# Five engine orders instead of one: a per-engine order table, and waits moved to the first instruction that needs them

## The chip, the cores and the metric

One core of one Trainium2 chip. It has a matrix engine (TensorE, "PE", its weight loads "PEld"), a vector engine (VectorE, "DVE"), a scalar engine (ScalarE, "ACT"), a general engine (GpSimd, "POOL") and a queue engine (SyncE, "SP") that here only issues DMAs. The engines run side by side, each through its own fixed list of instructions, and meet only at semaphores. The metric is the device time of one execution in microseconds, median of several runs.

## The reference

The input x is 4 items of 256 tokens by 256 channels; each item has a context `ctx_1024` (256 x 128) and a side input. Four layers of gated cross attention and gated feed-forward follow. What each stage of the kernel computes for one item b:

```
s0     x += tanh(g0) * mamba(ctx, gate = layernorm(x))      # conv, softplus step, 16 states of a linear
                                                           # recurrence over 256 tokens, 256 channels
h1,r1  h = layernorm(x); route to 2 of 8 experts (softmax, top 2)
s1     x += tanh * (8 experts of width 176 weighted by the routing, and a shared one of 352), SwiGLU
s2     x += tanh * two smooth-quantised (int8-like) matmuls against the side input and the context
s3     x += tanh * ternary-weight SwiGLU, width 1024
s4,sa  x += tanh * attention, 16 heads of 128, keys and queries rms-normed, 256 context tokens
s5     x += tanh * ternary-weight SwiGLU with activations quantised to 8 bits and a norm between
s6     x += tanh * attention whose queries and keys both come from the context
s7     x += tanh * ternary-weight SwiGLU, width 1024, with an rms norm inside
```

The ternary weights are made on the chip from full ones, at the start.

## The kernel before

Everything is in float32 but for splits into two or three bf16 or fp32r parts where precision allows it. An item's 256 tokens are two tiles of 128 partitions. Each item passes the stages in turn, and three chains of work run at the same time, one item apart: **front** (s0 with its 16 states, then h1 and the routing r1), **middle** (s1, s2, s3, and for items 1 to 3 also s4) and **rest** (for item 0 s4; then attention sa, s5, s6, s7). Beside them, at the start, run the preparation of the ternary weights (`ternary`, `group_ternary`, `copy7`) and of one matrix product per head (`value_output`). Each chain has its own PSUM banks and scratch: front Z0, middle W0, W1, AT, rest SC, PT, OP, AR. Item b's s1 needs item b's routing and item b-1 to be out of the middle; attention of item b needs item b out of s4 and item b-1 out of s7.

s1 has 14 chunks: TensorE makes gate and up (`gu`), ScalarE the tanh, VectorE two products, GpSimd the expert's weight, TensorE the `down` (`dn`) into AT. The experts' weights per token are spread by six wide products (`wide`, with the 0/1 matrix `esel`), which ScalarE copies to SBUF (L838). s3 and s7 have 8 chunks each of the same kind, where ScalarE makes the high part (`hi`) and GpSimd the low part (`lo`, L620) of the product. s4 makes keys and queries of 16 heads (`kq`), sums their squares (`nq`), and ends with the norm on ScalarE and the split of it in three bf16 parts on VectorE (L1802 to L1811, called rk3). Attention per head: scale the key (L1823), scores, maximum, exp, normalise, transpose, product with the context, output. A state n of s0 takes a broadcast matmul (`bc`, L994) on TensorE, two exps on ScalarE (L803), product, scan and product on VectorE (L1551, L1557, L1563), and a sum on GpSimd (L585).

**What sets the order.** Each engine's list is written by `interleave`. A stage is a generator that yields a number ahead of each step; the step whose number is smallest is written next, and a number below the one before it in its chain is lifted to that one. The number comes from `place(part, b, x)`: x is the step's place within its part (for a head 5 + 0.42, for a state n + 0.7), and `PLAN[part][b]` is a piecewise linear curve that turns it into a position on an axis common to all parts. In the kernel before, one curve with 3 to 7 knots per part and item serves all five engines, so the chains are merged in nearly the same way on each. The numbers set only the order; nothing waits for a time. An engine whose next instruction waits for a semaphore holds back all that is written behind it.

Some steps yield a place, wait for a semaphore and then issue nothing before they yield the next place, so another chain's step may be written behind such a wait:

```python
                yield at4(b, 4)
                pe.wait_ge(*at(b, "s4.act", "hT"))
                for n in range(NH + 1):
                    yield at_head4(b, n)
```

The loads: SP fills a ring of three weight slots for s1 (ringT), two for keys and queries (ringQ), three for attention's output (ringM), and loads the items; GpSimd's queue fills four slots for s3 and s7 (ring37). Each refill waits until the slot's last reader is done, and stands in its engine's order by the same table.

Of the kernel before, what the change touches and what calls it, by code (L numbers as in the profile page):

```python
# [34 lines left out]
NST = 16  # L35
# [8 lines left out]
NH = 16  # L44
# [55 lines left out]
def build(nc, a, out, known=None):  # L100
    ctx = ExitStack()
    with ctx:
# [218 lines left out]
        def dma_sem(name):  # L321
            return o.sem(name)

        def spilled(eng, name, upto=3):
# [12 lines left out]

        PLAN = {
            "s0": [((0, -20.36), (3.75, 4.35), (7.5, 20.16), (11.25, 25.48), (15, 28.91)), ((0, 122.84), (3.75, 130.98), (7.5, 130.99), (11.25, 136.34), (15, 143.71)), ((0, 265.28), (3.75, 265.29), (7.5, 272.7), (11.25, 276.6), (15, 286.71)), ((0, 482.81), (3.75, 488.87), (7.5, 492.24), (11.25, 497.42), (15, 507.8))],
            "state": [((-1.2, 24.56), (2.23, 42.06), (5.66, 57.57), (9.09, 64.79), (12.52, 83.32), (15.95, 95.39)), ((-1, 138.91), (2.39, 155.35), (5.78, 165.87), (9.17, 178.45), (12.56, 190.58), (15.95, 201.99)), ((-1, 281.56), (2.39, 292.6), (5.78, 297.26), (9.17, 398.88), (12.56, 427.98), (15.95, 456.95)), ((-1, 506.66), (2.39, 518.34), (5.78, 538.45), (9.17, 560.89), (12.56, 615.87), (15.95, 630.24))],  # L340
# [7 lines left out]
            "head": [((-0.25, 323.15), (4.312, 340.37), (8.875, 359.4), (13.44, 381.2), (18, 403.98)), ((-0.25, 498.6), (4.312, 540.92), (8.875, 569.31), (13.44, 592.16), (18, 614.38)), ((-0.25, 714.54), (4.312, 739.64), (8.875, 747.6), (13.44, 769.36), (18, 790.57)), ((-0.25, 1032.63), (4.312, 1036.64), (8.875, 1036.65), (13.44, 1121.71), (18, 1225.71))],  # L348
# [8 lines left out]
        def place(part, b, x):  # L357

            knots = PLAN[part][b]
            if x <= knots[0][0]:  # L360
                return knots[0][1] + (x - knots[0][0])
            for (x0, t0), (x1, t1) in zip(knots, knots[1:]):
                if x <= x1:
                    return t0 + (x - x0) * (t1 - t0) / (x1 - x0)
            return knots[-1][1] + (x - knots[-1][0])
# [1648 lines left out]
```

## Time and profile before

| | us |
|---|---|
| median of 3 runs (lowest, highest) | 1147.06 (1143.35, 1147.12) |
| profiled execution, its own time | 1148.34 |
| its span | 1146.6 |
| busy: PE / DVE / ACT / POOL | 837.9 / 760.7 / 523.6 / 322.3 |
| mean granted clock of TensorE | 0.852 |

### The profile page before, as it was taken

How to read it: one execution, taken by the hardware profiler on the slowest of the kernel's cores; microseconds unless marked ns; L12 is line 12 of the kernel's file. 1: busy time of each engine (PE TensorE's matmuls, PEld its weight loads, DVE VectorE, ACT ScalarE, POOL GpSimd, SP SyncE). 2: the span in 40 equal slices, each digit the busy share in tenths (PEclk: the TensorE clock that was granted, in tenths of full speed). 3: DMA queues.
4: the chain of work that ended last, by engine and by line, in shares of the span. 5: the costliest groups of instructions: out<-in, count | busy, mean ns of one | idle time of the engine just before them, and what ended most of it. 6: DMA issues, size and time to landing. Idle time of an engine off the chain costs nothing.

```text
span 1146.6 us, 12868 instructions
## 1 busy us (share of the span) xinstructions
PE 837.9 (73%) x3924; PEld 624.4 (54%) x3924; DVE 760.7 (66%) x1812; ACT 523.6 (46%) x1244; POOL 322.3 (28%) x394
## 2 busy tenths in 40 slices
PE   3111676646998977589799885898998769899455
PEld 2000355325666855357578664576886646667234
DVE  5898789874366787955688989554558654355542
ACT  5544543213554544455554553465344435556223
POOL 1433054403132103513444115224110331500204
PEclk9555589759999999789799998898999879989657
DMA  6511524424222202212323104124320221400002
GB/s 219 184 55 51 188 96 147 157 68 146 69 98 97 69 19 69 69 49 90 120 79 108 54 28 120 42 83 142 100 68 28 74 83 42 133 25 23 1 0 65
DMA packets 45476, 96.24 MB, mean 84 GB/s; under 512 B 4824, under 2 KB 16480, under 8 KB 44256
## 3 DMA queue, kind: packets, MB, share of 16 engines
q1 hardware_dynamic: 36192, 70.26, 19.0%
q0 software_dynamic: 9216, 25.17, 7.6%
q8 instruction: 32, 0.52, 0.2%
q14 instruction: 36, 0.29, 0.1%
HBM read 85.97 MB, written 9.44 MB: 83 GB/s over the span
## 4 chain that ended last, share of the span: by engine, by line
PE 45%; DVE 31%; issue 10%; ACT 9%; POOL 5%; DVEq 0%; POOLq 0%; ACTq 0%
PE bk L994 33%; PE bk L1045 7%; DVE ssm_u L1557 6%; DVE ssm_u L1563 2%; DVE ssm_u L1551 2%; PE bk L1240 2%; PE bk L1038 1%; DVE mx L1775 1%; DVE lnbuf L1465 1%; DVE t1A L1586 1%; DVE arB L1788 1%; PE bk L1376 1%; ACT arB L885 1%; DVE t2A L1589 1%; DVE t1B L1871 1%
## 5 line engine op out<-in xcount | busy, mean ns | idle before, releaser
L585 POOL TENSOR_TENSOR sy<-sy,ssm_u 128x512 f32<-128x512 f32 x64 | 86.6, 1354 | 110.6 <-DVE ssm_u L1563 104.2
L994 PE MATMUL bk<-hTA,ringT 128*128 128x256 f32 x448 | 116.6, 407 | 1.1 <-ACT hTB L769 0.7
L994 PE MATMUL bk<-bc,sel 96*128 96x512 bf16 x64 | 29.4, 463 | 97.3 <-DVE ssm_u L1563 93.6
L994 PEld LDWEIGHTS bk<-hTA,ringT 128*128 128x128 f32 x448 | 90.6, 207 | 17.5 <-issue 2.0
L557 POOL TENSOR_TENSOR lnbuf<-lnbuf,mhalf 128x2 f32<-128x2 f32 x32 | 23.4, 730 | 263.9 <-DVE lnbuf L1471 263.9
L1557 DVE TENSOR_TENSOR_SCAN ssm_u<-ssm_da,ssm_u 128x512 f32<-128x512 f32 x64 | 91.1, 1424 | 4.3 <-DVE ssm_u L1551 0.5
L994 PE MATMUL bk<-qk 128*128 128x256 f32 x288 | 80.4, 404 | 6.0 <-ACT arB L885 3.2
L885 ACT ACTIVATE arB<-bk,nb,rqs 128x256 f32<-128x256 f32 x128 | 71.0, 562 | 27.6 <-DVE nb L1778 27.4
L994 PE MATMUL bk<-arB,cx 128*128 128x256 f32 x256 | 69.5, 394 | 11.8 <-DVE qk L1823 8.9
L600 POOL TENSOR_TENSOR arA<-t2A,arA 128x256 f32<-128x256 f32 x44 | 38.0, 865 | 130.2 <-DVE t2A L1589 113.9
L803 ACT ACTIVATE ssm_da<-sdl,nega 128x255 f32<-128x255 f32 x128 | 57.1, 499 | 34.0 <-DVE ssm_u L1557 30.8
L920 ACT ACTIVATE arB<-bk 128x512 f32<-128x512 f32 x64 | 38.2, 597 | 70.2 <-PE bk L1240 70.1
L994 PEld LDWEIGHTS bk<-bc,sel 96*128 96x128 bf16 x64 | 6.3, 100 | 115.6 <-DVE ssm_u L1563 110.1
L810 ACT ACTIVATE thA<-bk 128x256 f32<-128x256 f32 x56 | 21.5, 383 | 103.3 <-PE bk L994 102.6
L1045 PE MATMUL bk<-ringM,arB 128*128 128x256 f32 x256 | 66.3, 381 | 1.2 <-ACT arB L929 0.9
L994 PEld LDWEIGHTS bk<-qk 128*128 128x128 f32 x288 | 54.4, 199 | 20.9 <-issue 8.5
L1045 PE MATMUL bk<-ringT,arA 128*128 128x256 f32 x224 | 59.4, 388 | 4.0 <-ACT arA L838 2.8
L1775 DVE TENSOR_REDUCE mx<-bk 128x2 f32<-128x512 f32 x68 | 46.7, 686 | 23.0 <-PE bk L994 22.8
L994 PEld LDWEIGHTS bk<-arB,cx 128*128 128x128 f32 x256 | 45.1, 191 | 30.5 <-issue 12.3
L1586 DVE SCALAR_TENSOR_TENSOR t1A<-thA,bk 128x256 f32<-128x256 f32 x88 | 36.5, 415 | 37.8 <-ACT thA L810 37.3
L994 PE MATMUL bk<-t2A,ringQ 128*128 128x256 f32 x192 | 54.1, 408 | 0.7 <-ACT t2A L769 0.7
L1551 DVE TENSOR_TENSOR ssm_u<-bk,sdu 128x512 f32<-128x512 f32 x64 | 43.9, 685 | 14.1 <-PE bk L994 13.7
(326 smaller groups left out, 2249.4 us busy)
## 6 DMA issues: line engine op xcount, KB each, us to landing
ringT<-in_w SPq DMA_DIRECT2D x56, 384.0 KB, 3.0
ring<-q3s POOLq DMA_DIRECT2D x32, 384.0 KB, 3.3
ringQ<-in_wqk SPq DMA_DIRECT2D x32, 384.0 KB, 2.9
ring<-q7s POOLq DMA_DIRECT2D x32, 384.0 KB, 3.3
ringM<-m4s SPq DMA_DIRECT2D x32, 256.0 KB, 2.6
q3s<-qk SPq DMA_DIRECT2D x4, 512.0 KB, 7.7
q7s<-qk SPq DMA_DIRECT2D x4, 512.0 KB, 4.3
qk<-in_wo SPq DMA_DIRECT2D x4, 512.0 KB, 4.6
```

What stands on the lines that cost most here:

```text
L557: g.tensor_tensor(lnr, lnv, mhalf[:, 0:2], ALU.pow).then_inc(*sig(f"{k}.pool", "lnr"))
L585: g.tensor_tensor(sy[:, :, :], sy[:, :, :], two(ssm_u[:, n % 3, :]), ALU.add).then_inc(*sig("s0.pool", "y", n))
L600: g.tensor_tensor(ac[:, p % 3, :], t2A[:, p % 3, :], wb[:, c, :], ALU.mult).then_inc(*sig("s1.pool", "act", p))
L803: i = s.activation(ssm_da[:, n % 2, e, 1:], sdl[:, e, 1:], ACT.Exp, scale=nega[:, e, n:n + 1])
L885: s.activation(pm[:, t, :], bank[:, t * S:t * S + S], ACT.Exp, bias=nb4[:, n, t:t + 1], scale=scale(t), accum_out=den4[:, n, t:t + 1]).the ...
L920: s.activation(pT4[:, (i - 1) % 2, :, :], halves(PT), ACT.Copy).then_inc(*sig("sa.act", "pT", i - 1))
L994: return t_.matmul(dst, lhsT, rhs, start=start, stop=stop)
L1045: i = t_.matmul(half(bank, t), lhsT[:, t * P:t * P + P], rhs, start=(c == 0 and j == 0 and t == 0), stop=(c == last and j == len(parts) - ...
L1551: v.tensor_tensor(two(ssm_u[:, n % 3, :]), both(n, 0), sdu[:, :, :], ALU.mult).then_inc(*sig(K, "bx", n))
L1557: v.tensor_tensor_scan(row, ssm_da[:, n % 2, :, :].rearrange("p e t -> p (e t)"), row, 0.0, ALU.mult, ALU.add).then_inc(*sig(K, "scan", n))
L1586: v.scalar_tensor_tensor(out=T1_[k][:, c % 2, :], in0=TH[k][:, c % 2, :], scalar=1.0, in1=bank[:, 0:S], op0=ALU.add, op1=ALU.mult).then_in ...
L1775: v.tensor_reduce(mx4[:, n, :], halves(bank), AXX, ALU.max).then_inc(*sig(K, "mx", j))
```

## The change

**The table.** `PLAN` now has a level more: engine, part, item. Each engine writes its name in `now[0]` ahead of its steps, and `place` reads `PLAN[now[0]]`. The curves have up to 44 knots, most at steps of that engine, so each engine has its own merge of the chains. Past its last knot a curve is now flat. The whole table is new; the units of its axis are not those of the old one (it runs to 2762 instead of 1226), and only the order within an engine matters. Its core, for the places that are spoken of below:

```diff
+        now = [None]
         PLAN = {
...
-            "kq": [((0, 259.93), (5.667, 277.58), (11.33, 289.41), (17, 310.1)), ((0, 432.3), (5.667, 446.88), (11.33, 466.85), (17, 485.44)), ((0, 642), (5.667, 648.37), (11.33, 676.61), (17, 700.12)), ((0, 814.39), (5.667, 841.53), (11.33, 861.43), (17, 898.83))],
-            "head": [((-0.25, 323.15), (4.312, 340.37), (8.875, 359.4), (13.44, 381.2), (18, 403.98)), ((-0.25, 498.6), (4.312, 540.92), (8.875, 569.31), (13.44, 592.16), (18, 614.38)), ((-0.25, 714.54), (4.312, 739.64), (8.875, 747.6), (13.44, 769.36), (18, 790.57)), ((-0.25, 1032.63), (4.312, 1036.64), (8.875, 1036.65), (13.44, 1121.71), (18, 1225.71))],
...
+            "pe": {
...
+                "kq": {0: ((0, 965.62), (3.52, 974.64), (4, 976.65), (4.52, 1090.51), (5, 1092.60), (5.52, 1100.46), (6, 1100.47), (6.52, 1106.84), (7, 1111.94), (7.52, 1117.22), (8, 1120.89), (8.52, 1124.44), (9, 1124.75), (9.52, 1131.76), (10, 1131.77), (10.52, 1134.83), (13, 1140.76), (13.52, 1142.14), (16.52, 1149.64), (16.9, 1149.95),),
+                    1: ((0, 1218.27), (1, 1298.78), (3, 1313.18), (3.52, 1374.12), (7, 1379.78), (7.52, 1379.89), (8, 1382.65), (9, 1386.85), (11, 1395.16), (11.52, 1401.08), (14, 1405.71), (14.52, 1405.72), (15.52, 1408.69), (16.52, 1408.80), (16.9, 1465.07),),
...
+                "state": {0: ((-1.2, 86.20), (-0.2, 90.21), (0.8, 195.15), (1.8, 197.16), (2.8, 205.74), (3.8, 210.25), (4.8, 338.83), (5.8, 347.35), (6.8, 347.36), (10.8, 349.93), (12.8, 386.64), (16, 386.65),),
...
+                    2: ((-0.2, 1094.28), (0.8, 1104.31), (2.8, 1113.45), (3.8, 1118.80), (4.8, 1122.52), (7.8, 1137.00), (9.8, 1147.45), (10.8, 1374.18), (11.8, 1377.35), (12.8, 1385.09), (13.8, 1402.75), (14.8, 1407.52), (16, 1455.35),),
+                    3: ((-0.2, 1653.94), (0.8, 1672.19), (1.8, 1699.25), (2.8, 1717.04), (3.8, 1729.33), (4.8, 1739.36), (5.8, 1750.21), (6.8, 1784.22), (8.8, 1792.33), (11.8, 1809.26), (12.8, 1814.66), (13.8, 1820.57), (16, 1833.12),)},
...
+            "dve": {
...
+                "kq": {0: ((16.7, 1153.57), (17, 1153.58),),
+                    1: ((16.7, 1470.93), (17, 1475.34),),
+                    2: ((16.7, 1832.84), (17, 1837.25),),
+                    3: ((16.7, 2160.25), (17, 2276.26),)},
...
+            "act": {
...
+                "experts": {0: ((0, -194.10), (1, -194.09), (2, -42.38),)},
...
+            "pool": {
...
+                    2: ((0.7, 2031.46), (11.4, 2067.05), (17.12, 2077.41), (17.2, 2077.42), (18.55, 2129.72), (23.48, 2129.73), (24.91, 2129.74), (27.8, 2129.75),),
...
+            "sp": {
...
         def place(part, b, x):
 
-            knots = PLAN[part][b]
+            knots = PLAN[now[0]][part][b]
             if x <= knots[0][0]:
                 return knots[0][1] + (x - knots[0][0])
             for (x0, t0), (x1, t1) in zip(knots, knots[1:]):
                 if x <= x1:
                     return t0 + (x - x0) * (t1 - t0) / (x1 - x0)
-            return knots[-1][1] + (x - knots[-1][0])
+            return knots[-1][1]
```

In TensorE's table, attention of item 0 starts at 1155.34 and the last `down` of item 1's s1 (x = 14.56) has 1134.26; attention of item 1 starts at 1694.24, item 2's s1 ends at 1668.89. In VectorE's, the residual after the states (x = 17 of "state") has 1473.20 for item 2 and 1833.57 for item 3.

**The waits.** Where a step held only a wait, the wait now stands behind the place of the first instruction that needs it:

```diff
                 transpose_h(b, "s4", h, bank)
-                yield at4(b, 4)
-                pe.wait_ge(*at(b, "s4.act", "hT"))
                 for n in range(NH + 1):
                     yield at_head4(b, n)
+                    if n == 0:
+                        pe.wait_ge(*at(b, "s4.act", "hT"))
```

The same is done on TensorE for `bc3` ahead of the states, `wT` ahead of the wide products, `hTl` in s3 and s7, and `qT` in s5; on ScalarE for `dl` ahead of the states and for item b-1's scores ahead of s4; on GpSimd for `yd`. `weights2` has places of its own instead of those of s1. SP gets a place of its own for two loads that wait for an earlier item:

```diff
                 if b >= 2:
+                    yield at_head(b - 2, NH + 1)
                     sp.wait_ge(*at(b - 2, "sa.pe", "o", NH - 1))
                 load(cxk[b % 2][:, :, :], "cx", b, f"cx{b % 2}")
```

`experts` (esel), `copy7`, `spill7` and `fill37` have parts of their own in the table, and two places in s5 move by 0.1 and 0.2. No instruction is added or taken away, and each chain's own order on each engine stays as it was.

## Rows read from the trace of the kernel before

**Rows 1.** Stretches: us, busy of each engine (instructions), TensorE's granted clock, DMA share, GB/s.
```profile
0.00:111.00 111.00, 24.24 (x56) 10.79 (x56) 91.23 (x124) 52.69 (x72) 36.01 (x44) 0.63 0.39 128
282.00:1000.00 718.00, 605.54 (x2974) 466.55 (x2972) 474.02 (x1215) 354.72 (x904) 204.39 (x257) 0.93 0.26 79
282.00:391.00 109.00, 100.64 (x427) 74.97 (x426) 61.64 (x136) 57.71 (x136) 25.02 (x25) 0.97 0.29 95
472.00:549.00 77.00, 60.28 (x297) 43.76 (x295) 48.58 (x121) 38.47 (x101) 24.25 (x33) 0.89 0.23 73
780.00:858.00 78.00, 73.08 (x366) 62.85 (x365) 39.82 (x109) 32.11 (x84) 15.98 (x23) 0.96 0.32 97
895.00:1000.00 105.00, 82.63 (x430) 62.79 (x430) 50.63 (x136) 51.53 (x130) 36.86 (x56) 0.88 0.30 88
1000.00:1146.60 146.60, 99.57 (x468) 72.01 (x468) 68.30 (x201) 55.13 (x156) 22.99 (x34) 0.77 0.07 22
```

**Rows 2.** Timeline, TensorE, 470 to 494: start, us, instruction [idle before, releaser].
```profile
481.00 0.61 PE L994 MATMUL bk<-bc,sel 96*128 96x512 bf16 x1 [7.54 <-DVE ssm_u L1563]
...
489.40 0.61 PE L994 MATMUL bk<-bc,sel 96*128 96x512 bf16 x1 [5.24 <-DVE ssm_u L1563]
```

**Rows 3.** Timeline, VectorE, 470 to 492.
```profile
473.50 2.70 DVE L1557 TENSOR_TENSOR_SCAN ssm_u<-ssm_da,ssm_u 128x512 f32<-128x512 f32 x1
...
480.86 1.68 DVE L1477 TENSOR_SCALAR hA<-xR,lnbuf 128x256 f32<-128x256 f32 x2
```

**Rows 4.** Timeline, TensorE, 690 to 720.
```profile
697.52 0.39 PE L994 MATMUL bk<-bc,sel 96*128 96x512 bf16 x1 [4.12 <-DVE ssm_u L1563]
...
716.06 1.11 PE L1092 MATMUL bk<-ident,ssm_u 128*128 128x128 f32 x4 [4.39 <-DVE ssm_u L1575]
```

**Rows 5.** Timeline, VectorE, 688 to 720.
```profile
709.57 2.94 DVE L1557 TENSOR_TENSOR_SCAN ssm_u<-ssm_da,ssm_u 128x512 f32<-128x512 f32 x1
```

**Rows 6.** Waits of TensorE, 282 to 1000: total us, times, longest.
```profile
PE bk L1045 <- POOL aclA L620: 16.1, 12, 3.8
```

**Rows 7.** Timeline of routing (item 0), rk3 (item 2), and the wide copies (item 3).
```profile
111.27 0.75 DVE L1465 BATCH_NORM_STATS2 lnbuf<-xT 128x6 f32<-128x256 f32 x2
...
112.70 0.73 POOL L557 TENSOR_TENSOR lnbuf<-lnbuf,mhalf 128x2 f32<-128x2 f32 x1 [4.34 <-DVE lnbuf L1471]
...
127.95 0.60 ACT L838 ACTIVATE arA<-bk 128x512 f32<-128x512 f32 x1 [0.70 <-PE bk L994]
...
783.57 0.29 DVE L1802 CAST arA<-arA 96x256 bf16<-96x256 f32 x1 [2.96 <-ACT arA L911]
...
786.22 0.22 DVE L1811 COPY rk<-arA 32x256 bf16<-32x256 bf16 x1
...
L838 ACT ACTIVATE arA<-bk x6: 378/597/598, 790.1 to 798.1; 128x512 f32<-128x512 f32 x5, 128x256 f32<-128x256 f32 x1
```

**Rows 8.** Stretches, columns as in rows 1.
```profile
240.00:260.00 20.00, 9.44 (x34) 6.35 (x35) 11.98 (x49) 2.84 (x9) 1.25 (x2) 0.50 0.00 1
480.00:500.00 20.00, 13.14 (x50) 9.26 (x50) 10.24 (x21) 6.96 (x19) 5.80 (x7) 0.65 0.06 21
540.00:580.00 40.00, 32.05 (x146) 23.69 (x145) 27.41 (x72) 23.13 (x51) 19.46 (x24) 0.82 0.35 107
700.00:720.00 20.00, 11.48 (x60) 8.16 (x58) 18.26 (x33) 6.45 (x18) 11.49 (x15) 0.67 0.36 100
780.00:800.00 20.00, 15.07 (x74) 12.23 (x73) 8.09 (x21) 9.90 (x20) 7.96 (x12) 0.83 0.42 122
```

**Rows 9.** Start: SP and ScalarE on the timeline, and line 728: min/median/max ns.
```profile
1.24 0.42 SPq L398 DMA_DIRECT2D cxT<-in_cxT  x1
...
9.87 0.60 ACT L774 ACTIVATE xpad<-bk 128x512 f32<-128x512 f32 x1 [1.19 <-PE bk L994]
...
L728 ACT ACTIVATE esel<-ident x3: 1357/1371/1374, 40.8 to 78.6; 32x1408 bf16<-32x1408 f32 x2, 8x1408 bf16<-8x1408 f32 x1
```

**Rows 10.** Line 1557, the scan: min/median/max ns, first and last start.
```profile
L1557 DVE TENSOR_TENSOR_SCAN ssm_u<-ssm_da,ssm_u x64: 1210/1225/2940, 36.4 to 709.6; 128x512 f32<-128x512 f32 x64
```

More of the change, by code:

```diff
@@ new lines, in build @@
+            "pool": {
[37 rows of a table added]
+                "state": {0: ((0.95, -166.65), (1.95, -133.34), (2.95, -131.33), (3.95, 113.25), (4.95, 219.36), (5.95, 221.37), (6.95, 222.18), (11.95, 224.39), (12.95, 296.70), (13.95, 296.71), (15.95, 373.02),),
[3 rows of a table added]
+            },
+            "sp": {
+                "copy7": {0: ((0.5, 455.38), (1.5, 550.59), (2.5, 643.97),)},
+                "group": {0: ((-9, 127.39), (7, 268.80), (23, 276.81),)},
+                "head": {0: ((3.69, 1171.08), (7.69, 1265.33), (9.69, 1265.34), (15.69, 1303.85), (17.69, 1303.86),),
[20 rows of a table added]
+                "ternary": {0: ((0.6, 197.30), (1.6, 225.41), (2.6, 303.61), (3.6, 330.12), (5.9, 340.23),)},
+                "vo": {0: ((-1, 590.23), (1, 596.70), (3, 599.00), (5, 615.51), (8, 721.97), (9, 721.98),)},
+            },
@@ L373, in build @@
         at_chunk = lambda b, n: place("s1", b, n)
-        at_w2 = lambda b, i: at_chunk(b, 8 + 0.3 * i)
+        at_w2 = lambda b, i: place("w2", b, i)
         at2 = lambda b, i, step: place("s2", b, 15 * i + step)
@@ L394, in _ @@
         def _(sp):
+            now[0] = "sp"
             flat = lambda r: r.rearrange("p a b -> p (a b)") if len(r.shape) == 3 else r
@@ L406, in load0 @@
                 if b >= 3:
+                    yield at6(b - 3, AT6["qk"] + 0.5)
                     sp.wait_ge(*at(b - 3, "s6.pe", "qk"))
@@ L497, in spill7 @@
                 for n in range(3):
-                    yield at_group(n, 10)
+                    yield place("copy7", 0, n + 0.5)
                     sp.wait_ge(*at(None, "prep.act", "q7", n))
@@ L526, in _ @@
         def _(pool):
+            now[0] = "pool"
             g = nc.gpsimd
@@ L681, in fill37 @@
                 for k, (st, b, c) in enumerate(ORDER37):
-                    if k < N37:
-                        yield at_group(1, 0)
-                        if k == 0:
-                            spilled(pool, "q3s")
-                    else:
+                    yield place("fill37", 0, k)
+                    if k == 0:
+                        spilled(pool, "q3s")
+                    if k >= N37:
                         pst, pb, pc = ORDER37[k - N37]
-                        yield at_sw[pst](pb, 5 + 2.8 * (pc + 1) + 2)
                         pool.wait_ge(*at(pb, f"{pst}.pe", "dn", pc))
@@ L698, in _ @@
         def _(act):
+            now[0] = "act"
             s = nc.scalar
@@ L724, in experts @@
                 for i in range(3):
-                    yield at_state(0, 2 + 4 * i)
+                    yield place("experts", 0, i)
                     n = 32 if i < 2 else NE
@@ L750, in copy7 @@
                 for n in range(3):
-                    yield at_group(n, 9)
+                    yield place("copy7", 0, n)
                     act.wait_ge(*at(None, "prep.dve", "q7", n))
@@ L990, in _ @@
         def _(pe):
+            now[0] = "pe"
             t_ = nc.tensor
@@ L1084, in s0 @@
                     yield at_state(b, n - (0.2 if k == 1 else 1.2))
+                    if n == 0:
+                        pe.wait_ge(*at(b, "s0.dve", "bc3"))
+                        if b == 0:
+                            pe.wait_ge(*at(None, "prep.act", "sel", 2))
+                            pe.wait_ge(*at(None, "prep.pool", "identb"))
                     if n >= k:
@@ L1115, in wide @@
             def wide(b):
-                yield at_wb(b, -0.1)
-                pe.wait_ge(*at(b, "r1.act", "wT"))
-                if b == 0:
-                    pe.wait_ge(*at(None, "prep.act", "esel", 2))
-                elif b - 1 in EARLY4:
-                    pe.wait_ge(*at(b - 1, "s4.dve", "rqs"))
-                else:
-                    pe.wait_ge(*at(b - 1, "s3.dve", "x", 1))
                 for j in range(NCR // 2 + 1):
@@ L1128, in wide @@
                         pe.wait_ge(*at(b, "r2.act", "wbe", j - 1))
+                    else:
+                        pe.wait_ge(*at(b, "r1.act", "wT"))
+                        if b == 0:
+                            pe.wait_ge(*at(None, "prep.act", "esel", 2))
+                        elif b - 1 in EARLY4:
+                            pe.wait_ge(*at(b - 1, "s4.dve", "rqs"))
+                        else:
+                            pe.wait_ge(*at(b - 1, "s3.dve", "x", 1))
                     for c in range(2 * j, min(2 * j + 2, NCR)):
@@ L1202, in swiglu @@
                 transpose_h(b, k, hA if k == "s3" else hB, AT if k == "s3" else OP)
-                yield pl(b, 4.5)
-                pe.wait_ge(*at(b, f"{k}.dve", "hTl"))
                 def slot(c):
@@ L1214, in swiglu @@
                     yield pl(b, 5 + 2.8 * c)
+                    if c == 0:
+                        pe.wait_ge(*at(b, f"{k}.dve", "hTl"))
                     ring_wait("ring37", N37, AT37[k, b, c])
@@ L1347, in s5 @@
                     yield at5(b, AT5["g"](c))
+                    if c == 0:
+                        pe.wait_ge(*at(b, "s5.act", "qT"))
                     t, f = c // 4, c % 4
@@ L1398, in _ @@
         def _(dve):
+            now[0] = "dve"
             v = nc.vector
```

68 lines of the change are left out of this document (42 added, 26 removed), and 200 rows, old and new, of the table PLAN.

## The prediction

> **What bounds the kernel now.** I read the stretches cut at stage boundaries first, then what TensorE waited for, then the instructions inside the gaps that these waits name. The stretches show three parts [rows 1]. Up to 111 us there is item 0's state recurrence and the weight preparation alone: VectorE 91.2 of 111 us, TensorE 24.2. From 1000 us there is only item 3's tail (attention, s5, s6, s7): 146.6 us with nothing beside it, and its steps follow each other in both tables. Between 282 and 1000 us three chains run together: TensorE is busy 605.5 of 718 us, VectorE 474. From 282 to 391 TensorE is full (100.6 of 109), from 780 to 858 nearly (73.1 of 78). So an order can only win the other 113 us, and must do it where TensorE is thin: 472 to 549 (60.3 of 77), about 700 to 720, 895 to 1000 (82.6 of 105).
>
> **Saturated part: no gain.** The new table moves item 1's s1 ahead of most of item 0's keys and queries (s4) and holds item 0's attention back until that s1 is over (on TensorE, attention starts at place 1155.34 and item 1's s1 ends at 1134.26; before, 323.15 and about 348). That permutes matmuls in a stretch that is full. I put 0 on it, -5 to +5 for the edges.
>
> **Gap 1, item 2's states beside item 0's s5.** TensorE stands 7.54 us and then 5.24 us for VectorE's product of one state [rows 2], 12.8 us in all. Behind the second of these matmuls the keys and queries of item 1 are queued, whose input hA VectorE had begun at 480.86 [rows 3], nine us before. In TensorE's new table the first four of them stand ahead of state 11 (kq 3 has place 1313.18, state 11 has 1374.18), so they fill the gap as soon as hA is there. What is late next is hA itself: residual, statistics 1.4 (111.27 to 112.70), GpSimd's power 0.73 [rows 7] and the applying are some 3.5 us, of which other work covers half. I take -11 (bounds -12.8 and 0: VectorE has all its work still to do, and it is VectorE that TensorE waited for).
>
> **Gap 2, the last states of item 3.** The same stall costs 4.12 us at 697.5 and 4.39 us at 716.1 [rows 4]. The new table puts states 0 to 6 of item 3 beside attention and the rest beside keys and queries of item 2, so that matmuls of another chain stand between two of them. 8.5 us go, about 3.5 us for the norm ahead of s4 come: -5 (bounds -8.5 and +3).
>
> **Gap 3, the low part in s3.** TensorE waited 16.1 us, 12 times, for GpSimd's subtraction in s3 [rows 6]. In items 1 and 2, s3 now runs beside attention, with one to four attention steps between its chunks. Half of it goes: -8 (bounds -16 and +4).
>
> **Gap 4, 895 to 1000 us.** TensorE is idle 22.4 of 105 us [rows 1]. GpSimd's table now takes the fifth gain of s5 and its square root (places 2077.41 and 2077.42) ahead of s3's last two low parts (from 2080.01), so item 2's s5 ends sooner, and TensorE takes s5's first transposes ahead of item 3's s4. s6 and s7 then lie beside more of the keys and queries. I take half of the idle: -11 (bounds -22 and +6: on VectorE the residual of s3 now stands behind s5's quantising, and item 3's s4, hence the tail, hangs on it).
>
> **What the new order costs: routing.** On VectorE the step rk3 of items 1 and 2 has place 1470.93 and 1832.84, and the residual after the states of items 2 and 3 has 1473.20 and 1833.57. So that residual, and behind it the next item's routing, waits until keys and queries are all normed. All three chains are then where TensorE has little to do: s6 in one, routing in another, and the third waits for routing's wide weights. The length: rk3 2.9 (783.57 to 786.44), a residual of about half a us, from statistics to the first wide copy 17.3 (111.27 to 128.55), six wide copies 8.4 (790.1 to 798.5) [rows 7]: 29 us. TensorE has some 16 us of matmuls for it by my count of s6, the end of s5, the first two chunks of s1 and the wide products, an estimate from their busy times in this trace; so 13 us are bare each time. Before, the same places had 8.0 idle us (540 to 580) and 4.9 (780 to 800) [rows 8]. That is +5 and +8: +13; bounds 0 and +35, the latter if those 16 us aren't ready in time.
>
> **Start.** ScalarE now builds esel first: two copies of 1.37 us stand before xpad, where it idled 1.19 us, and the third behind it [rows 9]: +1.5, and +1 for what the third delays. Item 1's two loads, some 0.4 us of issue each [rows 9], stand ahead of the small weights that everything waits for: +0.8. weights2 of item 0 moves on VectorE from about 180 us to about 18 us, loaded both times: 0. Sum +3.5 with rounding (0 to +6).
>
> **Moved waits.** A wait by itself blocks an engine only if steps of another chain are queued between it and its first instruction. In the old order I count none between on ScalarE, and on TensorE nine places with one or two steps (as a `down` of attention behind s3's wait for hTl); none of these is among the longer waits. -1 (0 to -5). SP: the refills of ringQ for item 3's first keys and queries now stand ahead of the last of ringM for item 2's attention, which are needed only after; 0, at worst one landing of about 3 us.
>
> **VectorE beside GpSimd.** The scan takes 1.225 us at the median [rows 10], but 2.70 us at 473.5 [rows 3] and 2.94 us at 709.6 [rows 5], in stretches where GpSimd sums sy and applies s5's gain. The new table puts nine states of item 3 beside item 1's s5, where there were five. Four more chances of 1.5 us, half of them hit: +3 (0 to +11). The Trainium skill, SBUF — State Buffer, section "Who interferes with whom", gives the cause: GpSimd and VectorE share one pair of ports, an exclusive lock. The trace agrees in kind (2.70 us for 1.225). If by that rule all nine states met a GpSimd instruction, the term would be nine times 1.5, some 13 us, and the sum ten higher.
>
> **Sum.** -11 - 5 - 8 - 11 + 13 + 3.5 - 1 + 3 = -16.5, against the profiled execution's 1148.34 us (span 1146.6): 1131.8. That execution is 1.3 us above the median of 1147.06; shifted by that and rounded: 1131 us.
>
> **Rivals.**
> *A, slower: the routing bubble.* Its place is from the last norm of s4 in items 1 and 2 to the first wide product of the next s1. If s6 and s1's first chunks aren't ready (on VectorE and ScalarE their steps are queued behind rk3 too), all 29 us are bare; against 8 and 5 before, that is +21 and +24, so 45 for my 13: 1131 + 32 = 1163. It decides from some 22 bare us per item. For it: from 240 to 260, where item 1's routing stands beside s2 alone, TensorE is busy 9.4 and VectorE 12.0 of 20 us [rows 8]. Against it: s6 needs nothing from routing. The granted clock is 0.50 in that stretch, the lower level of 1.2 GHz, and 0.65 from 480 to 500, but 0.96 from 780 to 858 where TensorE is full [rows 1, 8]. The Trainium skill, TensorE: Matmul & The Clock Gate, Part 1, has it as a rule: the low clock is the default, activity releases it. By this the 16 us of matmuls in each bubble would run slow for a part, up to 16 us more each time.
> *B, slower: balance lost.* Before, s5 with states filled VectorE (18.3 of 20 at 700 to 720 [rows 8]), and keys and queries came after, with s6, s7 and routing in their shade. Now both loads must overlap step by step. The old stretch 472 to 549 needed 77 us for 60.3 of TensorE [rows 1], a factor of 1.28; if the two new ones (some 50 us of TensorE each) have that where I assumed 1.12, each is 8 longer, and gaps 1 and 2 (16) are not won: 1131 + 32, 1163 again, with routing as forecast. It decides if the two stretches together exceed 135 us.
> *C, same.* The gaps only move: 1 to 4 are won at half (-17.5) and the costs stand (+18.5): 1148.
> *D, much faster.* An order of its own for each engine takes out half of the 113 idle us between 282 and 1000, since nothing is queued behind the wrong chain any more: 56 off, 18.5 on, about 1109. Against it: much of the idle is latency inside a chain.
>
> **How the numbers follow.** The forecast (1120 to 1140) has 0.29, D 0.18, C 0.16, A 0.22, B 0.15. A measurement of this kernel can tell about 0.5%, 5.7 us, from no change, so faster is below 1141.3. Faster is forecast, D and a little of C: 0.48; same 0.15; slower 0.37. The range goes from D's slower half, 1100, to past A and B, 1178.
>
> **What would show it.** Right: no wait over 3 us of L994's successor for the state product after 282 us; item 1's s1 ends some 25 us before 391 with a full TensorE; GpSimd as releaser of s3's `down` under 9 us in all; the tail from item 3's first scores 140 to 147 us as before. Wrong: TensorE idle over 20 us after the keys and queries of item 1 or 2 (A); VectorE over 90% with TensorE under 75% beside s5 (B); a start more than 6 us later.

## The result and the profile after

The changed kernel takes **1112.3 us** (median of 4 runs, 1111.38 to 1114.79), the kernel before 1145.55 in the same comparison: a ratio of 0.970, 95% interval 0.9675 to 0.9728. The forecast was 1131, with a gain of 16.5; the gain is 33, twice that. The range held it, the likeliest case did not: the time is that of rival D (1109), which had 0.18. The profiled executions have spans of 1109.6 and 1146.6 us, so the traces differ by 37.0; 3.7 of that is only which executions were traced (before's lies 2.8 us above its median, after's 0.9 below).

The first view is again the stretches, cut where the middle chain's stages begin and end by each trace: item 1's first gate, end of its s1, of its s3, of its keys and queries, item 2's first gate. Columns as in [rows 1]. Of the kernel before there follow the whole middle, then item 1's s1, its s2 and s3, its keys and queries, then s2 and s3 of item 2 and of item 3, and last the 30 us around item 3's routing ([rows 8] has item 2's):

```profile
282.20:1000.50 718.30, 605.34 (x2974) 466.45 (x2971) 474.25 (x1216) 354.72 (x904) 204.39 (x257) 0.93 0.26 79
282.20:392.80 110.60, 102.24 (x437) 76.45 (x435) 62.73 (x138) 59.02 (x140) 25.02 (x25) 0.97 0.30 95
392.80:477.00 84.20, 62.13 (x336) 48.11 (x334) 70.71 (x183) 39.24 (x105) 22.57 (x29) 0.94 0.21 59
477.00:555.20 78.20, 61.41 (x292) 44.75 (x293) 47.10 (x127) 40.85 (x103) 22.47 (x30) 0.87 0.23 74
637.30:714.70 77.40, 57.56 (x319) 44.01 (x317) 69.95 (x183) 37.96 (x100) 23.48 (x30) 0.94 0.23 67
858.50:926.80 68.30, 52.77 (x290) 41.04 (x289) 51.08 (x158) 30.43 (x86) 15.88 (x24) 0.90 0.21 60
776.00:806.00 30.00, 25.07 (x129) 20.27 (x128) 13.52 (x35) 16.25 (x38) 9.83 (x15) 0.89 0.47 142
```

and of the kernel after the same six stretches, then those around the routing of items 2 and 3:

```profile
287.20:962.80 675.60, 594.87 (x2975) 456.89 (x2973) 463.11 (x1212) 352.03 (x904) 205.04 (x257) 0.94 0.28 83
287.20:360.40 73.20, 68.44 (x295) 51.35 (x294) 46.82 (x89) 35.62 (x83) 26.83 (x25) 1.00 0.33 101
360.40:453.00 92.60, 81.96 (x437) 63.68 (x437) 68.86 (x194) 53.89 (x142) 15.52 (x19) 0.96 0.23 69
453.00:508.70 55.70, 48.56 (x217) 32.51 (x217) 43.46 (x104) 36.45 (x90) 18.85 (x23) 0.94 0.32 97
585.20:671.00 85.80, 71.52 (x383) 55.99 (x384) 75.27 (x195) 43.38 (x120) 23.73 (x28) 0.92 0.24 73
817.60:895.20 77.60, 63.17 (x352) 50.01 (x350) 60.30 (x187) 37.85 (x105) 16.93 (x25) 0.93 0.17 48
498.00:538.00 40.00, 29.40 (x129) 21.59 (x129) 27.89 (x90) 16.37 (x34) 4.14 (x5) 0.79 0.10 32
722.00:752.00 30.00, 21.05 (x102) 14.38 (x100) 23.11 (x80) 14.17 (x30) 5.15 (x6) 0.81 0.08 27
```

Length less TensorE's busy time is its idle time. Between item 1's first gate and the end of item 3's keys it falls from 113.0 to 80.7 us: 32.2. The same 2975 matmuls are busy for 594.9 and not 605.3 us: 10.5. The start is 5.0 longer (287.2 for 282.2), the tail 0.7. That is 37, all of it. Of the 32.2, the stretch of item 1's s2 and s3 gives 11.4 (22.1 to 10.6), item 2's 5.6 (19.8 to 14.3), item 3's 1.1, item 1's s1 3.6 (8.4 to 4.8), its keys and queries 9.7 (16.8 to 7.1).

What TensorE waited for between 287.2 and 962.8, total us, times, longest; L1796 is L1563 of before, L852 is L620 and L1710 is L1477:

```profile
PE bk L1271 <- DVE hA L1710: 9.8, 4, 5.3
PE bk L1325 <- DVE ssm_u L1808: 7.7, 2, 3.9
PE bk L1227 <- ACT arA L1069: 6.5, 10, 0.7
PE bk L1227 <- DVE qk L2055: 5.1, 9, 1.1
PE bk L1278 <- POOL aclA L852: 4.2, 5, 1.2
...
PE bk L1278 <- POOL aclB L852: 1.9, 2, 1.5
PE bk L1227 <- DVE ssm_u L1796: 1.8, 4, 0.6
```

Against [rows 6] GpSimd's low part costs 4.2 us, not 16.1. The state product costs 1.8; before it was 19.9 in the same stretch, both stalls of [rows 2] and the first of [rows 4] in it. The second of [rows 4] has not closed: the transposes behind item 3's last state (L1092 before, L1325 after) waited 4.39 us and now wait 3.77, and behind item 2's last state stands a new wait of 3.90. The wait for the norm's result hA has grown, from 5.8 us in four waits to 9.8 in four. On the timeline the broadcasts of item 2's states 13 and 14, which had stood 7.54 and 5.24 us, now find their input ready; so does that of state 15:

```profile
480.44 0.38 PE L1227 MATMUL bk<-bc,sel 96*128 96x512 bf16 x1
...
490.01 0.39 PE L1227 MATMUL bk<-bc,sel 96*128 96x512 bf16 x1
...
497.12 0.38 PE L1227 MATMUL bk<-bc,sel 96*128 96x512 bf16 x1
...
503.12 1.11 PE L1325 MATMUL bk<-ident,ssm_u 128*128 128x128 f32 x4 [3.90 <-DVE ssm_u L1808]
...
728.12 1.11 PE L1325 MATMUL bk<-ident,ssm_u 128*128 128x128 f32 x4 [3.77 <-DVE ssm_u L1808]
```

### The profile page after: what moved, and what is told of

It is laid out like the page before. It is cut to its first block, busy times and chain, and to the rows that moved or that the text cites. A ratio compares the mean times of both kernels' runs of the same rounds, so it can differ in the third digit from the quotient of the medians.

```text
span 1109.6 us, 12862 instructions
## 1 busy us (share of the span) xinstructions
PE 829.2 (75%) x3924; PEld 618.0 (56%) x3924; DVE 751.4 (68%) x1812; ACT 520.3 (47%) x1244; POOL 317.2 (29%) x394
## 3 DMA queue, kind: packets, MB, share of 16 engines
q1 hardware_dynamic: 36192, 70.26, 19.8%
## 4 chain that ended last, share of the span: by engine, by line
PE 41%; DVE 30%; issue 13%; POOL 8%; ACT 6%; DMA 1%; SPq 0%; POOLq 0%; DVEq 0%; ACTq 0%
PE bk L1227 28%; PE bk L1278 7%; DVE ssm_u L1790 5%; DVE ssm_u L1784 2%; PE bk L1472 2%; POOL sy L817 2%; POOL arA L832 2%; DVE ssm_u L1796 2%; DVE mx L2007 1%; PE bk L1271 1%; ACT arB L1116 1%; DVE lnbuf L1698 1%; DVE arB L2020 1%; PE bk L1608 1%; PE bk L1572 1%
## 5 line engine op out<-in xcount | busy, mean ns | idle before, releaser
L817 POOL TENSOR_TENSOR sy<-sy,ssm_u 128x512 f32<-128x512 f32 x64 | 83.2, 1301 | 131.3 <-DVE ssm_u L1796 130.6
L1227 PEld LDWEIGHTS bk<-hTA,ringT 128*128 128x128 f32 x448 | 91.1, 206 | 16.5 <-ACT hTA L1000 1.1
L1790 DVE TENSOR_TENSOR_SCAN ssm_u<-ssm_da,ssm_u 128x512 f32<-128x512 f32 x64 | 87.1, 1360 | 4.0 <-ACT ssm_da L1034 0.3
L1227 PE MATMUL bk<-qk 128*128 128x256 f32 x288 | 80.7, 407 | 4.9 <-ACT arB L1116 3.7
L1116 ACT ACTIVATE arB<-bk,nb,rqs 128x256 f32<-128x256 f32 x128 | 71.0, 560 | 21.1 <-DVE nb L2010 20.7
L1278 PE MATMUL bk<-ringT,arA 128*128 128x256 f32 x224 | 62.5, 403 | 12.9 <-POOL arA L832 12.4
L1278 PEld LDWEIGHTS bk<-ringT,arA 128*128 128x128 f32 x224 | 42.1, 199 | 28.0 <-POOL arA L832 19.8
L1227 PE MATMUL bk<-t2A,ringQ 128*128 128x256 f32 x192 | 51.1, 390 | 0.7 <-ACT t2A L1000 0.7
```

The lines of the kernel that those rows point to most:

```text
L817: g.tensor_tensor(sy[:, :, :], sy[:, :, :], two(ssm_u[:, n % 3, :]), ALU.add).then_inc(*sig("s0.pool", "y", n))
L1116: s.activation(pm[:, t, :], bank[:, t * S:t * S + S], ACT.Exp, bias=nb4[:, n, t:t + 1], scale=scale(t), accum_out=den4[:, n, t:t + 1]).the ...
L1227: return t_.matmul(dst, lhsT, rhs, start=start, stop=stop)
L1278: i = t_.matmul(half(bank, t), lhsT[:, t * P:t * P + P], rhs, start=(c == 0 and j == 0 and t == 0), stop=(c == last and j == len(parts) - ...
L1790: v.tensor_tensor_scan(row, ssm_da[:, n % 2, :, :].rearrange("p e t -> p (e t)"), row, 0.0, ALU.mult, ALU.add).then_inc(*sig(K, "scan", n))
```

## The experiments

**The moved waits and a ladder of tables.** All of these have the code of the change, and both tables in it. `old` maps a place into the table of before, `new` into that of the change; a cut by part and item, the same for all engines, says which orders come first. A step behind the cut gets 10000 more, so nothing behind the cut can be written ahead of it:

```diff
+        def place(part, b, x):
+            # old_order: return old(part, b, x), without a cut
+            ahead = x < 12 if part == "fill37" else b <= AHEAD.get(part, 0)
+            return new(part, b, x) if ahead else 10000 + old(part, b, x)
+            # old_to_item1, old_start: old and new exchanged
```

> The moved waits alone: every engine's instructions in the order of before, but for seven bc and one s1 matmul group on TensorE and a few lines on ScalarE; the waits stand where the change puts them. Theory P (the order of item 1's stretch makes the gain): 1143 to 1147, as before, since no instruction comes earlier. Theory W (the moved waits let engines through that stood behind a wait): 1130 or less.

Measured 1133.66 us, ratio 0.9889 (0.9851 to 0.9927). Theory P missed by 9, W by nearly 4: with nearly no instruction moved, 13 us are gone.

> The new table for everything up to item 0's s3 and item 1's states and routing, the old one behind that. Theory P: the start costs the 4 to 5 us that the first gate of item 1's s1 is later in the trace (287.2 for 282.2), so 1149 to 1152. Theory E (an order of its own for each engine gains a little everywhere): a quarter of the gain is here, 1138.

1137.53 (0.9903 to 0.9950): against old_order the start costs 3.9, near the 4 to 5 that P gave it. P's range (1149 to 1152) missed by 11 all the same, as it left out the moved waits, and that the time falls on E's 1138 is luck: E had a quarter of the table's gain here, and there is none.

> The new table up to the end of item 1's keys and queries, item 2's states and item 0's s5; the old order for all that follows. Theory P: item 1's stretch was 47 us shorter, so with the 5 of the start and with item 0's s6 and s7 now ahead of item 2's s1 (up to 10), 1105 to 1118. Theory E: a little over half of the path is done, 1128 to 1135.

1140.38 (0.9922 to 0.9959). Both missed, P by more than 20, E by 5. Item 1's stages are as short as in the change: its keys end at 506.5, where new_start has 545.7. But item 2's first gate is at 551.3, there 550.2. The row between:

```profile
506.50:551.30 44.80, 31.06 (x144) 25.11 (x143) 23.91 (x79) 14.02 (x37) 13.59 (x21) 0.71 0.21 59
```

Item 0's s6 and s7 are still to do, and the old order puts them ahead of item 2's s1: 44.8 us with 13.7 idle at clock 0.71, where the change has 8.6. How much of this is a debt of the order ahead, and how much comes of the seam where two tables that weren't made for each other meet, the run doesn't separate.

> The new table up to the end of item 2's keys and queries, item 3's states and item 1's s5, the old order behind that. Theory L (what item 1's order brings forward is a loan: the middle chain is 37 us ahead at that cut and the rest chain as far behind, and at the cut the old order runs item 0's s6 and s7 with nothing beside them; it pays only if the next item's order takes it up): the same debt is due here, 20 to 30 us, so 1132 to 1140. Theory S (the gain comes in the items 2 and 3 by their own orders, about half in each): 1122 to 1128.

1131.25 (0.9829 to 0.9896), 0.75 under L's range and 3 over that of S. The same debt stands one item later:

```profile
731.10:773.30 42.20, 31.10 (x148) 25.93 (x149) 21.18 (x69) 13.21 (x38) 15.18 (x23) 0.75 0.19 53
```

> The other way round: the old order up to the end of item 1's keys and queries (and item 2's states and item 0's s5), the new table behind that. Theory S: items 2 and 3 give their 28 us with no help from item 1, 1133.7 - 28 = 1106 to 1112. Theory L: without item 1's order there is nothing for the new table to take up, 1125 to 1140.

1135.68 (0.9874 to 0.9946): L. The new table behind item 1 alone gives nothing over old_order; in front of it alone it costs; both together give 25. So what item 1's stages are shortened by is, by these runs, largely a loan from the other chain, which the next item's order has to take up; each of them has a seam of its own as well (here 15.3 us, from 524.3 to 539.6, with 8.2 busy).

**The start on its own.**

> The changed kernel with the old order for the start (all of the preparation, item 0 up to s3, item 1's states and routing). If the start costs what new_start had over old_order (1137.5 - 1133.7 = 3.9): 1107 to 1110. If item 1's order needs the new start: 1112 or more.

1108.06, ratio 0.9672 (0.9642 to 0.9701), as expected from the first pair: 4.2 less than the change, and the best version of all. Against old_order, which has the same code and the same start, it stands 25.6 lower: that is what the table behind the start is worth. The two middle stretches, old_order's first:

```profile
284.50:985.30 700.80, 597.44 (x2973) 463.26 (x2971) 471.70 (x1216) 354.10 (x904) 204.42 (x257) 0.94 0.27 81
387.90:472.00 84.10, 63.26 (x336) 49.45 (x334) 70.08 (x182) 39.16 (x105) 22.54 (x29) 0.88 0.21 60
```

```profile
281.90:957.00 675.10, 594.30 (x2975) 455.81 (x2973) 463.74 (x1216) 351.38 (x904) 204.81 (x257) 0.95 0.27 83
355.70:448.20 92.50, 81.93 (x437) 63.60 (x436) 68.80 (x194) 53.74 (x142) 15.55 (x19) 0.96 0.22 69
```

Idle 103.4 against 80.8, so 22.6 of the 25.7 in the middle are idle time; 10.3 of them lie in item 1's s2 and s3 (20.8 to 10.6).

**One wait alone.** What in old_order gave 13 us? In the kernel before, `yield at4(b, 4)` ahead of the wait has the number 438.72 for item 1, and `at_head4(1, 0)` only 432.3, so the first keys and queries were lifted to 438.72, behind the broadcast of state 14 of item 2. Two edits of the kernel before:

```diff
 # wait_s4
-                yield at4(b, 4)
-                pe.wait_ge(*at(b, "s4.act", "hT"))
                 for n in range(NH + 1):
                     yield at_head4(b, n)
+                    if n == 0:
+                        pe.wait_ge(*at(b, "s4.act", "hT"))
 # wait_place
-                yield at4(b, 4)
+                yield at4(b, 3)
```

> The kernel before with one of the moved waits alone, TensorE's for hT ahead of s4. On TensorE this puts one matmul elsewhere: the broadcast of item 2's state 14 stands behind the first keys and queries of item 1, not ahead of them. Theory G (the 5.24 us stall of gap 1 goes, and with it the rest of the chain comes earlier): 1139 to 1143, half of what the moved waits gave together; the broadcast of state 14 isn't waited for any more. Theory N (the stall only moves): 1146 to 1149.

1136.95 (0.9890 to 0.9939), two us under G's range: one matmul behind instead of in front of ready ones and one wait moved, and 10 us are gone. The stall ahead of state 13 is still there (6.63 us, before 7.54). But the broadcast that had stood 5.24 us [rows 2] finds its input there, and item 1's first keys start at 484.64, in the trace of before at 489.80:

```profile
484.64 1.13 PE L994 MATMUL bk<-t2A,ringQ 128*128 128x256 f32 x4 [0.69 <-ACT t2A L769]
...
489.49 0.38 PE L994 MATMUL bk<-bc,sel 96*128 96x512 bf16 x1
```

> The kernel before, its wait for hT still in a step of its own, but with the number at4(b, 3) and not at4(b, 4). Every engine's instructions are in the order of wait_s4; only the wait stands before the step that it stood before in the kernel before. Theory N4 (it was the number, which lifted the keys and queries behind the broadcast of state 14, and not the blocking of the wait): 1135 to 1139, as wait_s4. Theory W (the wait's blocking): nearer 1147.

1143.03 (0.9956 to 0.9987), between the two theories and clear of both. The number, and with it the order, gives 4 us (3 by the ratio); the wait's own place gives the other 6, and in the two traces all matmuls stand in the same order. In the profiled executions (spans 1138.0 and 1134.2) the middle is 707.0 long here, 702.6 in wait_s4; 1.8 of that is idle time, 2.6 is longer matmuls. Item 2's keys show both. This is wait_place, then wait_s4:

```profile
706.10:714.10 8.00, 4.86 (x20) 2.97 (x21) 4.95 (x13) 1.91 (x5) 3.48 (x5) 0.50 0.00 0
714.10:722.10 8.00, 8.00 (x32) 6.03 (x31) 6.62 (x17) 5.02 (x16) 2.00 (x3) 0.79 0.15 49
```

```profile
705.10:712.90 7.80, 5.50 (x22) 3.85 (x23) 5.58 (x14) 1.83 (x5) 3.35 (x5) 0.50 0.00 0
712.90:720.60 7.70, 7.70 (x36) 5.74 (x36) 5.74 (x16) 5.37 (x16) 2.00 (x3) 1.00 0.17 53
```

TensorE is fully busy in both second rows, at granted clock 0.79 (32 matmuls) and 1.00 (36). What the wait blocks stands just ahead. Behind the transposes of hA come eight matmuls of item 1's s5, which don't read hT, and only then the first keys. Again wait_place, then wait_s4:

```profile
710.47 1.42 PE L1038 MATMUL bk<-ident,hA 128*128 128x128 f32 x4 [0.93 <-DVE hA L1477]
712.58 0.61 PE L994 MATMUL bk<-q5g,arB 128*128 128x256 bf16 x2 [0.69 <-ACT t2A L769]
```

```profile
709.33 1.42 PE L1038 MATMUL bk<-ident,hA 128*128 128x128 f32 x4 [0.93 <-DVE hA L1477]
710.54 0.64 PE L994 MATMUL bk<-q5g,arB 128*128 128x256 bf16 x2
```

In a step of its own the wait stands ahead of the eight: they start 2.11 us after the transposes do and not 1.21. That is 0.9 us by the wait; the next few matmuls at the lower clock make it some 2, for item 2's keys are 72.0 us long in both kernels with the old wait (before, wait_place) and 69.8 and 69.7 in wait_s4 and old_order. Another 2 us of the traces' difference lie in item 1's first keys, where nothing stands between wait and keys: the same matmuls from 481.02 to 485.39 here, from 484.64 to 486.90 in wait_s4, at clocks of 0.54 and 1.00. Why the clock differs there, one trace of each can't say, nor where the rest of the 6 us lies.

**Is it the lag of the chains or the small order?** One curve for all engines, and the old small order at the new lags:

```diff
+        OLD = {...}                                   # one_curve*: fitted to the steps' end times after
+        def place(part, b, x): return old(part, b, x)
+        STEPS = {...}                                 # new_lags and all below: engine -> part -> item -> (x, us)
+        def place(part, b, x): return 10000 + curve(STEPS[now[0]][part][b], x, 0.1)
```

> One curve per part and item for all engines again, as in the kernel before (3 to 7 knots, fitted to when the steps of the changed kernel ended in its trace), the moved waits as in the change. So the chains stand to each other as in the change, but no engine has a merge of its own. Theory P (what counts is which stage lies beside which): 1110 to 1122. Theory E: the gain is lost, 1138 to 1150.

> One curve per part and item for all engines, 3 to 7 knots, fitted as in one_curve, but item 1's wide products now may go ahead of item 0's keys and queries, as in the change (in one_curve they had to stand behind them, which by its trace cost 85 us at that place: wide products of item 1 at 387 for 289). Theory P (which stage lies beside which counts): 1110 to 1125. Theory E (an order of its own for each engine counts): 1135 to 1155.

> The same with four times the knots (10 to 25 per part and item), one curve for all engines. Theory P: as one_curve2 or a little less, 1108 to 1120. Theory E: well above the change, 1130 to 1150. If this is near 1112 and one_curve2 is not, it is the fineness of the curves that counts and not that each engine has its own.

> From item 1's s1 on, each engine's order of before (its steps at the times they ended in the trace of old_order), but every chain stretched so that each stage of an item starts, is half through and ends when it did in the changed kernel: the same stretch for all engines. The start is the new one. So the stages lie beside each other as in the change, while the small order within them is the old one. Theory L (which stage lies beside which makes the gain): 1112 to 1122. Theory O (the small order of each engine makes it): 1132 to 1145, as new_start (1137.5) or worse.

Measured 1239.92, 1206.25, 1256.51 and 1201.07 us (ratios 1.082, 1.053, 1.094, 1.047), all far worse than either kernel and past what any theory gave. In new_lags the chains stand to each other nearly as in the change (item 1's s1, then s2 and s3, then its keys lie beside so much of the rest that TensorE has 303, 431 and 214 matmuls in them, in the change 295, 437 and 217), and TensorE still idles 143.8 us in the middle (80.7 in the change), 4.4 of them for weights on their way. Theories P and L fall: these lags with the old small order are worth nothing. The fits are crude, so that a well tuned single curve would lose as much is not shown; before's own single curve stands at 1133.66 with the moved waits. So whether it takes an order for each engine, or one curve as well fitted would do, stays open.

**How much a small shift costs.** The change's order, each engine's steps at the times at which they ended, and one chain shifted by a ramp:

```diff
+        # early_states: front, items 2, 3, up to -8, -6 us; front_early_2: -2 us
+        # middle_early_4: s1 to keys of item 1, -4 us; rest_early_20: item 0's last keys to s7, -20 us
+        # rebuilt: no shift
```

> The changed kernel with the front chain of items 2 and 3 earlier on each engine: item 2's last states and its routing by up to 8 us, item 3's by up to 6. In the change TensorE was idle 10.6 of 40 us around item 2's routing and 9.0 of 30 around item 3's. Theory R (the residual behind the last state and the routing behind it set the bubble): 6 to 12 us less, 1100 to 1106. Theory V (VectorE's load in those stretches sets it; what comes earlier delays keys and queries as much): 1110 to 1116.

> A control for new_lags and early_states: the changed kernel's order rebuilt in the same way, from the times at which each engine's steps ended in its trace, with no shift. TensorE's, VectorE's and ScalarE's orders are those of the change to the instruction; on GpSimd the refills for s3 and s7 stand a little elsewhere among its sums and products. If the shifts made the losses of those two: 1110 to 1116. If GpSimd's refills made them: 1120 to 1135.

> As early_states but by 2 us and not 8 (the front chain of items 2 and 3, all engines): 36 lines of TensorE's order differ from the change, 67 of VectorE's. Theory Q (what costs is a state's broadcast that stands ahead of another chain's ready matmuls, each time one to three us): between rebuilt and early_states, 1114 to 1124. Theory R: less than rebuilt by 2 to 4.

> The changed order with the rest chain of item 0 (end of s4, attention, s5) up to 20 us earlier on all engines, so that its first heads lie beside item 1's s1 again, as before the change: half way back to the old lag of these two chains. Theory L (heavy beside light: attention beside s2 and s3 fills TensorE): half of that gain goes, 1122 to 1130. If the lag doesn't matter: 1110 to 1116. Theory O (any shift breaks the fit of the orders): 1135 or more.

> The changed order with the middle chain of item 1 (s1 to its keys and queries) up to 4 us earlier in each engine's order, so that it goes first a little more often. Theory O: 1118 to 1130. Theory K (the middle chain is the one whose end starts the next item, so it should go first): 1104 to 1110.

> The order of new_start (old order behind the new start, 1137.5) with the middle chain of item 1 up to 4 us earlier, as middle_early_4 has it on the changed order, and further on to the end of its keys and queries. If any shift of one chain costs some 20 us (as from rebuilt to middle_early_4, 1116.7 to 1137.8) because the small order is tuned in both: 1150 to 1160. If the old order is slack: 1134 to 1141.

| run | us | ratio to before (95%) | against its control |
|---|---|---|---|
| rebuilt | 1116.74 | 0.9732 (0.9703, 0.9761) | change +4.4 |
| front_early_2 | 1120.72 | 0.9771 (0.9741, 0.9801) | rebuilt +4.0 |
| early_states | 1134.63 | 0.9884 (0.9857, 0.9911) | rebuilt +17.9 |
| middle_early_4 | 1137.79 | 0.9905 (0.9870, 0.9941) | rebuilt +21.1 |
| rest_early_20 | 1144.84 | 0.9982 (0.9958, 1.0007) | rebuilt +28.1 |
| old_middle_early_4 | 1149.48 | 1.0016 (0.9994, 1.0037) | new_start +12.0 |

The control shifts nothing, and its 4.4 us are DMA issues standing elsewhere: GpSimd's refills, and by its trace, which the expectation leaves out, some of SyncE's loads too, from 11 us on (the orders of TensorE, VectorE and ScalarE are the change's). It came out 0.7 over the range that I gave it. early_states is nearly 19 us past its nearer theory, V. R and K fall: in middle_early_4 item 1's s1 ends 1.5 us earlier than in the control (360.7 for 362.2), but its keys end 24 later (534.3 for 510.4). Q's range holds, and O for middle_early_4 (within 1118 to 1130 expected, 1137.8 measured, so by more than it said) and rest_early_20. Idle time in the stretch from item 1's first gate to the end of its keys, here for rebuilt, middle_early_4 and rest_early_20 in turn:

```profile
288.90:510.40 221.50, 198.93 (x947) 147.54 (x946) 159.14 (x385) 125.94 (x314) 61.22 (x67) 0.97 0.28 85
```

```profile
289.70:534.30 244.60, 205.66 (x944) 151.84 (x943) 161.26 (x384) 124.81 (x313) 62.09 (x66) 0.92 0.25 76
```

```profile
286.70:543.20 256.50, 212.40 (x982) 157.67 (x981) 164.28 (x408) 129.33 (x322) 63.65 (x69) 0.93 0.24 74
```

22.6 us idle become 38.9 and 44.1, and the clock falls from 0.97 to 0.92 and 0.93: 944 matmuls are busy for 205.7 us where 947 had 198.9. In early_states the state product stalls TensorE again, ten times in the middle for 11.9 us, where the change has four times for 1.8:

```profile
PE bk L1282 <- DVE ssm_u L1851: 11.9, 10, 2.7
```

```profile
464.78 0.39 PE L1282 MATMUL bk<-bc,sel 96*128 96x512 bf16 x1 [2.24 <-DVE ssm_u L1851]
...
472.17 0.39 PE L1282 MATMUL bk<-bc,sel 96*128 96x512 bf16 x1 [2.69 <-DVE ssm_u L1851]
```

The old order pays for a shift too, up to 12 us for a like one: new_start isn't rebuilt, so part of the 12 may be GpSimd's refills, which the shifted run has elsewhere. Both orders are tuned, the new one by this more finely. old_middle_early_4 came out half a us under the range that called any shift dear.

## Why the prediction was half of the gain

**Gap 1** was right in place and means: both stalls are gone from the trace. That its size fits is partly luck: -11 was forecast for both, and wait_s4 takes out the second, of 5.24 us, alone and gains 10, while the first still stands 6.63. And it was put to the table. It is the removed step `at4(b, 4)` that frees the keys and queries, already with the old order.

**Moved waits, -1: the step that failed first.** I asked what was queued between a wait and its first instruction. I didn't ask what the step's number does to the numbers behind it: an empty step lifts all later ones of its chain. That is 4 us by wait_place. The other 6 of wait_s4 go against my count itself, by which no such wait mattered: in item 2 it held back eight ready matmuls. Measured about -13 (old_order), gap 1's second stall in it.

**Gap 2**, -5, was half right: 4.12 us are gone, but the other 4.39 are still 3.77, and item 2 has a like wait of 3.90 that it hadn't; the norm's waits grew by 4.0, where I had put 3.5. **Gap 3**, -8, was right in kind: GpSimd's waits fell by 11.9. **Gap 4**, -11: item 3's s2 to keys lost 5.3 us of idle time (15.5 and 13.2 to 14.4 and 9.0). Half; over the last 105 us ahead of the tail, the stretch that I had read, it is 22.4 to 19.3.

**Saturated part, 0, and "an order can only win the other 113 us, where TensorE is thin: 472 to 549, 700 to 720, 895 to 1000".** This is the second step that failed. The full stretch and the thin one behind it are one sum: item 1's s1, s2 and s3 had 30.4 us idle in all and now have 15.4. Of the 30.4, TensorE's waits for GpSimd's low part are 6.8 and those for the state product 2.7; for the rest I had 0. The change takes item 0's attention from beside item 1's s1 (TensorE 102.2 of 110.6) to beside s2 and s3 (62.1 of 84.2 before, 82.0 of 92.6 after), and these 84 us, with 22.1 idle, were missing in my list of thin stretches. But that lag is not enough by itself, as new_lags shows.

**Routing, +13** was too dear: the idle time around it went from 8.0 [rows 8] to 10.6 us for item 2 and from 4.9 to 9.0 for item 3, +6.7 in all. The bubble is there (8.6 and 9.0 us between keys and the next gate, 4.2 and 3.1 before), and it is filled better than I counted. Rival A's point of decision, 22 bare us per item, is far off.

**Start, +3.5:** right. 3.9 and 4.2 by the two pairs; on ScalarE xpad's first copy stands at 12.22 and not 9.87 [rows 9].

**VectorE beside GpSimd, +3:** wrong in sign. The 64 scans took 1360 ns in the mean after, 1424 before, so 4 us less on VectorE; the longest is 2.3, not 2.9. Behind 282 us ten scans took over 1.3 us before and four after, in each trace all of them while a GpSimd operation ran. The slow scans are there, but more states beside s5 did not make more of them.

**No term at all** stood for the matmuls' own time. It is the third step that failed, a term put at nothing without a reason: 10.5 us of the 37 between the traces are the same matmuls in less time, at a granted clock of 0.94 for 0.93. I used the clock only against the change (rival A).

**The sum.** The runs give, in my terms: moved waits with gap 1 -13 against -12; start +4 against +3.5; everything else -25.5 against -8 (gaps 2 to 4 -24, routing +13, VectorE beside GpSimd +3). They add up to 34.5, a little over the 33 measured, since the runs had other executions of before beside them. The last difference is the error; that the first pair agrees is a coincidence, as only the table takes out gap 1's first stall. The traces divide the 37 another way. Idle time in the middle: forecast -20 (gaps -35, waits -1, routing +13, VectorE beside GpSimd +3), measured -32.2. The matmuls' own time: 0, measured -10.5. Start and tail: +3.5, measured +5.7. By the runs the 25.5 can't be divided by gap or by item. The nearest theory is rival D, "nothing is queued behind the wrong chain any more", which I took down to 0.18 because "much of the idle is latency inside a chain". The stretches of [rows 1] had 113 us idle; 32 went, where D had 56; with 10 us of shorter matmuls and cheaper costs it still came near D's time, which is luck in the number.

Of the signs that I named, all on the right side came: no state product over 0.6 us; item 1's s1 over at 360.4, 31 us before 391; GpSimd 6.1 us in s3's `down`; the tail as before (146.8 us from the end of the last keys). They could not tell 16 from 33: signs that a mechanism works don't measure it.

What stays open: which engine's own order gives how much of the 25 us (not tried), whether a single curve could give it, and most of wait_place's 6 us.

## What to carry to other kernels

An in-order engine makes a merge of chains brittle: one matmul placed ahead of ready ones cost 4 us, with a wait in the wrong step 10, and a shift of one chain by 4 us cost 21 on the new order, up to 12 on the old one. So judge an order by what stands right behind each instruction that has to wait, also an empty step whose number lifts the rest of its chain, and don't argue gaps one by one: count idle time over a full and a thin stretch together, since one feeds the other. When a stage gets shorter, look at once for the work of the other chain that it left behind, and for who takes it up. And give the clock a term: fewer stalls shorten the matmuls too.

## What the runs showed of the hardware

TensorE's busy time for the same 2975 matmuls between item 1's first gate and item 3's last key moves with the idle time around them: 594.3 us where 80.8 were idle (old_start, clock 0.95), 597.4 at 103.4 (old_order, 0.94), 605.3 at 113.0 (before, 0.93), 621.0 at 143.8 (new_lags, 0.91). So 63 us of idle time brought 27 more of busy time. Busy time times clock is 562 to 565 in all four, so within the rounding the clock accounts for it. It isn't a strict law: new_to_item2 has only 94.0 idle and 599.2 busy. Two kernels whose matmuls stand in the same order got clocks of 0.79 and 1.00 in nearly the same full stretch of 8 us, and of 0.54 and 1.00 in item 1's first keys, as shown above.
